# Message passes of a graph network kernel: folding, turning and finishing moved to different batches

## What is computed

```python
def spline_conv(x, row, col, basis, idx, W, b):
    z = jnp.einsum('ni,kio->nko', x, W).reshape(N * K, Fout)
    gathered = z[col[:, None] * K + idx]
    msg = jnp.einsum('es,eso->eo', basis, gathered)
    out = jax.ops.segment_sum(msg, row, num_segments=N)
...
h = jax.nn.elu(spline_conv(h, row, col, basis, idx, stn2_w, stn2_b))    # 64 -> 64 channels
...
return spline_conv(x, row, col, basis2, idx2, conv_w, conv_b)           # 32 -> 32 channels
```

## Time and profile before

| | us |
|---|---|
| median of 3 runs (15043.63 to 15060.23) | 15059.24 |
| the profiled execution | 15048.42 |
| its span in the trace | 15046.6 |

### The profile page before, as it was taken

The page is one execution under the profiler, slowest core; times in us unless marked ns, Lnnn a source line. Parts: engine busy times, 40 slices in busy tenths (PEclk is TensorE's granted clock), DMA queues, the critical chain, the costliest instruction groups (busy, mean ns, idle before and its releaser), DMA issues. The chain is left out here.

```text
span 15046.6 us, 161276 instructions
## 1 busy us (share of the span) xinstructions
PE 7175.2 (48%) x32826; PEld 6046.3 (40%) x32827; DVE 5601.9 (37%) x11348; ACT 1742.8 (12%) x5296; POOL 8945.7 (59%) x9011
## 2 busy tenths in 40 slices
PE   5200455556664545455557775444444453334333
PEld 1100344436663333444546665434333343333332
DVE  9300344444455666433335554333233351111111
ACT  0000233312220110000010001111111110000000
POOL 0667666636665555555526765666666526664666
PEclk9555666655557777555555555555555555555555
DMA  7990111123321111111111112000011121112111
GB/s 272 146 108 4 51 68 68 66 70 93 90 85 34 39 40 39 28 30 30 30 16 12 12 12 16 12 12 12 21 23 23 23 35 12 12 12 12 13 13 14
DMA packets 790415, 642.11 MB, mean 43 GB/s; under 512 B 363677, under 2 KB 680591, under 8 KB 790101
## 3 DMA queue, kind: packets, MB, share of 16 engines
q1 hardware_dynamic: 466836, 303.92, 10.7%
q0 software_dynamic: 295168, 243.14, 8.6%
q10 hardware_dynamic: 28288, 93.72, 1.6%
HBM read 265.07 MB, written 386.20 MB: 43 GB/s over the span
## 5 line engine op out<-in xcount | busy, mean ns | idle before, releaser
L801 PE MATMUL ps<-got,oh 128*128 128x33 f32 x7040 | 1663.9, 400 | 2361.9 <-DVE oh L624 813.5
L801 PEld LDWEIGHTS ps<-got,oh 128*128 128x128 f32 x7040 | 1572.4, 327 | 2521.2 <-issue 2507.2
L764 POOL DMA_INDIRECT got<-q_table,idx x1760 | 1814.8, 1031 | 1144.4 <-DVE idx L806 600.3
L2113 POOL DMA_INDIRECT msg<-msg,idx x1792 | 1758.3, 981 | 1206.5 <-DVE msg L2046 653.1
L764 POOL DMA_INDIRECT got<-h_table,idx x1760 | 1724.1, 980 | 1091.7 <-DVE idx L806 565.6
L1700 POOL DMA_INDIRECT cell<-rec,idx x880 | 921.8, 1047 | 590.2 <-ACT rec L1683 323.8
L347 POOL DMA_INDIRECT rec_r<-sc_rec,sc_idx x832 | 816.8, 982 | 765.4 <-ACT sc_rec L339 424.3
L1365 POOL DMA_INDIRECT rec_d<-rec,idx x880 | 911.7, 1036 | 534.9 <-ACT rec L1306 278.5
L1965 POOL DMA_INDIRECT cell<-rec,idx x880 | 896.5, 1019 | 486.4 <-issue 266.2
L624 DVE TENSOR_TENSOR oh<-iota_f,rd 128x512 f32<-128x512 f32 x1105 | 762.1, 692 | 968.4 <-DMA b<-in_L_gnn_b 394.7
L806 DVE CAST idx<-rd 128x4 int32 (+1 forms) x892 | 161.3, 182 | 2461.6 <-DMA got<-msg 588.4
(11 more groups left out here) (329 smaller groups left out, 13686.9 us busy)
## 6 DMA issues: line engine op xcount, KB each, us to landing
got<-rec_d SPq DMA_DIRECT2D x220, 416.0 KB
rec_d<-padd ACTq DMA_DIRECT2D x4, 11648.0 KB
rec_d<-padd ACTq DMA_DIRECT2D x4, 11232.0 KB
cin<-cell SPq DMA_DIRECT2D x225, 136.0 KB
msg<-msg,idx POOLq DMA_INDIRECT x1792
msg<-zpad SPq DMA_DIRECT2D x8, 3575.0 KB
got<-msg SPq DMA_DIRECT2D x220, 130.0 KB
cell<-rec,idx POOLq DMA_INDIRECT x1760
```

What stands on the lines that cost most here:

```text
L764: nc.gpsimd.indirect_dma_start(out=s["got"][:, n, g, :], out_offset=None, in_=table, in_offset=bass.IndirectOffsetOnAxis(ap=s["idx"][:, n, ...
L801: mm = nc.tensor.matmul(psum_rows[:, ds(at[g], W)], s["oh"][:, n, g, :], s["got"][:, n, g, 0:W], start=False, stop=False)
L2113: nc.gpsimd.indirect_dma_start(out=msgs, out_offset=bass.IndirectOffsetOnAxis(ap=idx[:, n, g:g + 1], axis=0), in_=msg[:, n, g, :], in_offs ...
```

## The change

The work of each step stays as it is; its place in the order of its engine changes.

- VectorE: in turn k it runs prepare(k+2) and then finish(k-1). Two batches are prepared ahead of the first turn. In the last turn, no batch is prepared beyond the end.
- ScalarE: the copy of batch 0 comes first; in turn k it runs idx(k) and then copy(k+1).
- TensorE: in turn k it runs turn_h(k+1) and then product(k).
- SyncE: the load of a batch beyond the end, and the wait for it, are gone.
- Some turns at the ends are written outside the loops: three of 56 on DVE, two on ACT, one on PE.

```diff
-                        load(K, TILES_C, 0)
-                        sp.wait_ge(loaded[0], 16 * (NIC + 1))
...
-                        prepare(0, 0, 0)
-                        def finish(i, first):
+                        def finish(i, n, k, first):
...
+                        def turn(i, first, last):
                             for n in range(R):
                                 k = i * R + n
-                                prepare(k + 1, i + (n + 1) // R, (n + 1) % R)
...
+                                if not last or n < R - 2:
+                                    prepare(k + 2, i + (n + 2) // R, (n + 2) % R)
+                                if n:
+                                    finish(i, n - 1, k - 1, first)
+                                elif not first:
+                                    finish(i - 1, R - 1, k - 1, isinstance(i, int) and i == 1)
+                            if last:
+                                finish(i, R - 1, K - 1, False)
...
+                        def copy_turned(k, n):
+                            act.wait_ge(s_turn, k + 1 + R)
+                            act.wait_ge(s_mul, k + R - 1)
+                            nc.scalar.sem_inc(tick, 1)
+                            nc.scalar.copy(hft[:, n % 2, :, :], ps[:, n % 2, :].rearrange("p (g e) -> p g e", g=G)).then_inc(s_copy, 1)
...
-                                act.wait_ge(s_turn, k + 1 + R)
-                                act.wait_ge(s_mul, k + R - 1)
-                                nc.scalar.sem_inc(tick, 1)
-                                nc.scalar.copy(hft[:, n % 2, :, :], ps[:, n % 2, :].rearrange("p (g e) -> p g e", g=G)).then_inc(s_copy, 1)
...
+                                if not last or n < R - 1:
+                                    copy_turned(k + 1, n + 1)
...
+                                if not last or n < R - 1:
+                                    turn_h(k + 1, (n + 1) % R, False)
                                 ids = block_ids(ENG.PE, "c", t, WMAX)
...
-                                turn_h(k + 1, (n + 1) % R, False)
```

More of the change, by code:

```diff
@@ L2029, in prepare @@
                                                     bcast(by.unsqueeze(3), [P, G, fold, F]), ALU.mult).then_inc(s_fold, 1)
-                        prepare(0, 0, 0)
-                        def finish(i, first):
+                        def finish(i, n, k, first):
+                            v.wait_ge(s_mul, k + 1 + R)
+                            by = pair[:, n, :, :] if fold == 2 else fb[:, n, :, 0, :]
+                            b0 = 2 + banks * (n % 2)
+                            y = ps[:, b0:b0 + banks, :].rearrange("p b m -> p (b m)")[:, 0:G * rest * F]
+                            nc.vector.tensor_tensor(wy[:, n % 2, :, :, :], y.rearrange("p (g c o) -> p g c o", g=G, c=rest),
+                                                    bcast(by.unsqueeze(3), [P, G, rest, F]), ALU.mult).then_inc(s_wy, 1)
+                            v.wait_ge(s_wy, k + 1 + R)
+                            if not first:
+                                v.wait_ge(sent[n], 16 * G * i)
+                                nc.vector.sem_inc(tick, 1)
+                            nc.vector.tensor_reduce(msg[:, n, :, 0:F], wy[:, n % 2, :, :, :].rearrange("p g c o -> p g o c"),
+                                                    AX.X, ALU.add).then_inc(s_msg, 1)
@@ L2049, in _ @@
-                        turns(v, NIC, finish)
+                                if not last or n < R - 2:
[6 more added lines that the diff above has]
+                                finish(i, R - 1, K - 1, False)
@@ L2051, in _ @@
+                        prepare(0, 0, 0)
+                        prepare(1, 0, 1)
+                        turn(0, True, False)
+                        turn(1, False, False)
+                        with v.Fori(2, NIC - 1) as i:
+                            turn(i, False, False)
+                        turn(NIC - 1, False, True)
                     @block.scalar
@@ L2053, in _, with number @@
                         nc.scalar.sem_inc(s_idx, R)
-                        def number(i, first):
+                        def copy_turned(k, n):
[3 more added lines that the diff above has]
+                            nc.scalar.copy(hft[:, n % 2, :, :], ps[:, n % 2, :].rearrange("p (g e) -> p g e", g=G)).then_inc(s_copy, 1)
+                        def number(i, first, last):
                             for n in range(R):
@@ L2081, in _, with turn @@
                             nc.tensor.sem_inc(sem, R)
-                        turn_h(0, 0, True)
-                        with pe.Fori(0, NIC) as i:
+                        def turn(i, last):
                             for n in range(R):
                                 k, t = i * R + n, i * STEP + n * G
+                                if not last or n < R - 1:
+                                    turn_h(k + 1, (n + 1) % R, False)
                                 ids = block_ids(ENG.PE, "c", t, WMAX)
@@ L2100, in _ @@
                                 mm.then_inc(s_mul, 1)
-                                turn_h(k + 1, (n + 1) % R, False)
+                        turn_h(0, 0, True)
+                        with pe.Fori(0, NIC - 1) as i:
+                            turn(i, False)
+                        turn(NIC - 1, True)
                     @block.gpsimd
```

18 lines of the change are left out of this document (5 added, 13 removed).

## The result

| | us |
|---|---|
| before, median of 4 runs (15043.63 to 15060.23) | 15058.97 |
| after, median of 4 runs (14925.22 to 14962.07) | 14957.30 |
| ratio, 95% interval | 0.9933 (0.9921 to 0.9945) |
| after, the profiled execution | 14925.22 |

A forecast was written before the change was run, and what follows sets the result against it. The prediction took POOL, often waiting for finished messages behind PE's late hand-overs, as the bound. Wins of 196 us (stage 1) and 43 (stage 2), sum 239, took 15048.4 to 14809, stated as 14815; range 14650 to 15020.

The forecast's parts named there:

- POOL's floor of 1.27 us a scatter: Both stages: a scatter takes POOL 0.97 + 0.30 us at best, 1137 us a stage; 647 us lie above it.
- The added wait of the product behind the turning: TensorE: product(k) queues behind turn_h(k+1)'s wait for the fold of k+1, which should be met as DVE folds earlier.
- ScalarE, SyncE and the turns outside the loops at 0: Copy behind idx(k), dropped load beyond the end, and turns written outside the loops (between 0 and 9 us): each taken as 0.
- The copy and the product leave stage 1's idle time: Stage 1: copy (0.58) and product (3.78) leave POOL's idle time; waits fall from 363 to about 180 us, longest to about 5.
- VectorE's order at 0: VectorE: prepare(k+2) ahead of finish(k-1) costs 0; a product's hand-over may be late by a batch more.
- The size, `to_cells`' pace of 1.498 us for both stages: Both stages reach the pace of `to_cells`, which already has this order: stage 1 wins 196 us, stage 2 43.
- third rival: Slower: serial late hand-overs delay the product 6.5 us, runs shrink from four batches to three in stage 2; 15136 us, chance 0.08.
- Stage 2 from 1.546 to 1.498, 43 us: Stage 2's share of the forecast: its time per scatter falls to the pace of `to_cells`, winning 43 us.
- second rival: Nothing comes: POOL runs dry after the same 16 scatters, idle some 4.4 us, whatever the order; 15048 us, chance 0.10.
- First rival: More comes: a deeper pipeline hides nearly all lateness, both stages at the gather's 1.429 us; 14685 us, chance 0.17.
- Runs of 20 and more, hand-overs 2 to 10 us late some 9 us into a run: Expected signs: runs of 20 and more scatters appear, while PE's hand-overs stay 2 to 10 us late some 9 us in.
- Wrong if the lateness itself grows with the run: Stated condition of failure: the prediction is wrong if hand-overs get later as runs of scatters get longer.

The follow-up runs named there:

- e6: The kernel before, unaltered, run again on a chip with prompt hand-overs: 13147.55 us.
- e5: The change, unaltered, run again on a chip with prompt hand-overs: 13121.62 us, ratio 0.9974 to the kernel before.
- e2: Kernel before with only TensorE's and ScalarE's part of the change, VectorE and SyncE in the old order, prompt hand-overs: 14059.18 us, ratio 1.0676.
- e10: Kernel before with only VectorE's and SyncE's part of the change, TensorE and ScalarE in the old order, late hand-overs: 14996.77 us, ratio 0.9966.
- e13: The change plus 16 increments of an unawaited semaphore on TensorE after every product, late hand-overs: 15335.69 us beside 15241.18 for the kernel before.
- e18: The change with all weights taken from one place, 6 of TensorE's 34 instructions a batch fewer, late hand-overs: 15112.13 us, ratio 0.9921.
- set A: The runs of the main result, late hand-overs: kernel before 15058.97 us, the change 14957.30; compared here is the trace of the kernel before.
- e16: The change plus 16 increments of an unawaited semaphore on ScalarE after every copy, late hand-overs: 15123.56 us beside 15173.05 for the kernel before.

## Why the prediction was right in direction and wrong in size

- **POOL's floor of 1.27 us a scatter**: right. In e6 and e5 both stages run at 1.277 to 1.282.
- **The added wait of the product behind the turning is met, since VectorE folds a turn earlier**: right, and it is the most expensive place of the change. With TensorE's and ScalarE's part alone it costs 6.8% (e2); with VectorE's part nothing.
- **ScalarE, SyncE and the turns outside the loops at 0**: right where it can be seen; e5's paces are within 0.002 of e6's.
- **The copy and the product leave stage 1's idle time**: right in part, and worth less than thought. The earlier trace rows show one of the longest waits; in 34 of the 58 long ones the product was already over when POOL ran dry. After the change 14 of 43 still hold the end of a product. An idle time is now some 3 us of waiting (median 3.04), `wy`, `msg` and 0.95 us to the start. The longest wait fell to 7.6 us, not to about 5, and the waits in stage 1 to 297 us, not to 180.
- **VectorE's order at 0**: right as a cost, missed as a gain. The prediction names the batch of room that a product gets and gives it no time, but it brings 58 of stage 1's 78 us (e10).
- **The size, `to_cells`' pace of 1.498 us for both stages**: this is the step that failed. `to_cells` was chosen because its work on TensorE is nearest. But a late hand-over comes when it comes, and then stage 1 must still run `wy` and `msg`, 3.1 us, which no order takes out of the idle time; `to_cells` has one copy of 0.27 us. And `to_cells` isn't alike otherwise: where nothing is late it runs at 1.345 us a scatter (e6), the two stages at 1.28. My own rows gave a better sum: a hand-over some 2.5 us after POOL falls idle, 3.1 of finish and 1.2 of steps behind each run of four or five batches, so 1.69 or 1.61. That it would be five is known only now. These terms stood in the earlier trace rows, and only the third rival used one of them. The term was 196 us and measured 78.
- **Stage 2 from 1.546 to 1.498, 43 us**: measured 24. The second rival, the same 16 scatters before POOL runs dry, is what happened there in 51 of 57 runs; it was given 0.10 for both stages together. Its fixed 4.4 us of idle time wasn't: the mean fell to 4.00.
- **First rival, both stages at the gather's 1.429**: it didn't come near.
- **Third rival, runs of three batches**: one run of 12 in stage 1 after the change, none in stage 2. Its premise fails too: in e10 43 of stage 2's 78 runs are 12 long, and the pace stays at 1.547, since the idle times are shorter as well (3.30 us in the mean).
- **Runs of 20 and more, hand-overs 2 to 10 us late some 9 us into a run**: seen in stage 1 (7.35 and 8.45 us late, above). "Wrong if the lateness itself grows with the run": the single hand-overs aren't later than the 10.1 us of before, but the one that POOL needs still comes 2.5 to 3.3 us after POOL falls idle. A run longer by a batch bought no earlier release.
- **That the lateness belongs to the program**: wrong, and stated nowhere as an assumption. It belongs to the condition that the chip is in. In the prompt condition there is almost nothing for this change to win: 0.9974 there, 0.9933 and 0.9945 in the late one.

## What stays open

What the late condition is. The runs show that it comes and goes on one chip, and that it lengthens the stretches in which GpSimd scatters or gathers (1854 of 1901 us) and hardly anything else. They show that it slows TensorE, SyncE and ScalarE, here and there GpSimd too, and that more instructions on an engine make it worse for that engine. On VectorE none shows, but none were added there. They don't show a queue. The Trainium skill ("NOTIFIC — the notification-queue block", "Overflow: three behaviours, one of which stalls the engine") describes one candidate: the block that takes the engines' trace records holds its producers back when its internal pipeline is full. The rows of e13 (16 increments at 51 ns, then one in 0.71 us) look like a queue that has filled. The missing records speak for this candidate as well, since two thirds of those of the semaphores are gone in just the late stretches; but a queue that only holds back would lose none, and both could follow from a third thing. e18 speaks weakly against a mere count of instructions. All executions here carried such records, so none tells whether one without them would be late. This is argued, not shown. A longer pause, rings of eight batches and TensorE's and ScalarE's part alone weren't tried in the late condition.

## What to carry to other kernels

Size a change to a pipeline from the cycle of its own waits (how long until the release, what must still run behind it, how much is queued ahead), not from the pace of a neighbouring stage whose finish is shorter. Count how often a wait looks like the one that you read: the one in the earlier trace rows was among the longest. When an engine's order is turned so that a product stands behind the next batch's turning, move the producer of that turning ahead in the same change; alone it made one stage three quarters slower. Before explaining a wait that ends at odd times, run the same kernel again: here 1.9 ms of 15 were a condition of the chip, and a change or a pause is worth something else in each. And look whether the trace is whole before you trust what it names as the end of a wait.

## What the runs showed of the hardware that was not expected

- The same kernel takes 13155 to 13164 us or 15054 to 15244 us (medians of the sets), on one chip at different times too.
- In the slower condition plain instructions on SyncE take 0.69 to 0.73 us each some microseconds into a run of indirect DMAs, instead of 0.02 to 0.05 (e6 against set A), and so do added increments on TensorE (e13) and ScalarE (e16). The increments are quick again while GpSimd is idle (17 ns in e16).
- The trace of the slower condition lacks two thirds of the semaphore records (65583 against 192944 for the same program), nearly all of them in the stretches of indirect DMAs.
- The hand-over for which GpSimd waits comes late enough that `wy` starts 2.5 to 3.3 us after GpSimd falls idle in stage 1 of the changed kernel, and 2.4 us in the median in stage 2.
- Indirect DMAs of 128 rows go out every 1.27 us at best, in either condition.
- 2.3 us of idle time for GpSimd in every 16 scatters makes the changed kernel 1.7% slower than the kernel before in one condition and 1.3% faster in the other.
